# Row tiles in two banks for the transposes and the inverse width DFT of a spectral convolution block

## What is computed

```
def _L0_conv_ref(x, w1_real, w1_imag, w2_real, w2_imag):
    xf = jnp.fft.rfft2(x, norm='forward')
    top = jnp.einsum('bixy,ioxy->boxy', xf[:, :, :hm0, :hm1], w1)
    bot = jnp.einsum('bixy,ioxy->boxy', xf[:, :, -hm0:, :hm1], w2)
    out_fft = out_fft.at[:, :, :hm0, :hm1].set(top)
    out_fft = out_fft.at[:, :, -hm0:, :hm1].set(bot)
    return jnp.fft.irfft2(out_fft, s=(h, w), norm='forward')
...
x = x + _L0_conv_ref(_ln_c(x), ...)
t = _to_tokens(x)
t = t + _L0_ffn_ref(_ln_t(t), ...)
x = _from_tokens(t, x)
x = x + _L1_conv_ref(_ln_c(x), ...)
t = _to_tokens(x)
t = t + _L1_ffn_ref(_ln_t(t), ...)
x = _from_tokens(t, x)
```

## Time and profile before

| | |
|---|---|
| median of 3 runs | 623.37 us (618.92 to 623.65) |
| the profiled execution | 616.65 us |
| its span, first to last instruction | 614.8 us |
| TensorE matmuls busy | 572.2 us, 93% of the span |
| TensorE weight loads busy | 532.8 us, 87% |
| VectorE busy | 340.9 us, 55% |
| ScalarE busy | 315.9 us, 51% |
| GpSimd busy | 63.8 us, 10% |
| mean granted TensorE clock | 0.967 of full speed |

### The profile page before, as it was taken

The page is one execution under the profiler, slowest core; times in us unless marked ns, Lnnn a source line. Parts: engine busy times, 40 slices in busy tenths (PEclk is TensorE's granted clock), DMA queues, the critical chain, the costliest instruction groups (busy, mean ns, idle before and its releaser), DMA issues.

```text
span 614.8 us, 25791 instructions
## 1 busy us (share of the span) xinstructions
PE 572.2 (93%) x10936; PEld 532.8 (87%) x10936; DVE 340.9 (55%) x825; ACT 315.9 (51%) x791; POOL 63.8 (10%) x62
## 2 busy tenths in 40 slices
PE   8979799999997999997999999999999999966897
PEld 7979799999996987896999999989999999956773
DVE  3647666656469725564544444434544445498326
ACT  4766556642287302344555555576665555668400
POOL 4000000020021000000000003520000044710000
PEclk9989999999998979998999999999999999997779
DMA  9830782150000000000000004430000344300007
GB/s 353 328 136 2 276 298 117 37 238 1 2 1 1 2 20 1 0 1 1 4 0 0 3 3 109 109 40 4 0 0 3 58 81 75 64 0 1 2 3 273
DMA packets 48155, 40.74 MB, mean 66 GB/s; under 512 B 42553, under 2 KB 42809, under 8 KB 46876
## 3 DMA queue, kind: packets, MB, share of 16 engines
q1 hardware_dynamic: 46606, 37.27, 18.7%
q0 software_dynamic: 1344, 2.17, 1.7%
q10 hardware_dynamic: 144, 0.39, 0.2%
HBM read 27.49 MB, written 4.19 MB: 52 GB/s over the span
## 4 chain that ended last, share of the span: by engine, by line
PE 74%; DVE 11%; ACT 6%; POOL 2%; DMA 2%; issue 2%; SPq 2%; ACTq 0%; DVEq 0%
PE PS L732 32%; PE PS L443 6%; PE PS L696 5%; PE PS L518 5%; PE PS L464 3%; PE PS L646 3%; PE PS L725 2%; PE PS L593 2%; PE PS L542 2%; PE PS L502 2%; DVE sums L1042 2%; PE PS L549 2%; PE PS L563 2%; DVE RCD L1054 2%; SPq L329 2%
## 5 line engine op out<-in xcount | busy, mean ns | idle before, releaser
L732 PE MATMUL PS<-RE,conv_sb 128*64 128x64 f32 x6048 | 228.9, 227 | 2.0 <-DVE RE L1154 1.5
L732 PEld LDWEIGHTS PS<-RE,conv_sb 128*64 128x64 f32 x6048 | 211.2, 137 | 11.1 <-DVE RE L1154 3.7
L1154 DVE SCALAR_TENSOR_TENSOR RE<-PS,RE 128x64 f32<-128x64 f32 x504 | 113.2, 225 | 122.0 <-PE PS L732 111.3
L725 PE MATMUL PS<-ones_bf,biasT 128*64 128x64 bf16 x1008 | 100.4, 192 | 0.0
L865 ACT ACTIVATE RE<-RCD 128x128 f32 (+1 forms) x126 | 38.9, 310 | 53.7 <-DVE RE L1154 53.6
L725 PEld LDWEIGHTS PS<-ones_bf,biasT 128*64 128x64 bf16 x1008 | 59.9, 112 | 0.8
L464 PE MATMUL PS<-warm 128*128 128x128 bf16 x540 | 42.5, 250 | 8.6 <-ACT RCD L840 4.5
L464 PEld LDWEIGHTS PS<-warm 128*128 128x128 bf16 x540 | 39.3, 114 | 9.9 <-ACT RCD L840 4.7
L318 POOL DMA_DIRECT2D RE<-RCD x32 | 18.6, 588 | 200.7 <-ACT RCD L868 200.7
L929 DVE TENSOR_REDUCE sums<-RE 128x32 f32<-128x1024 f32 x16 | 19.4, 1218 | 33.3 <-ACT RE L772 33.3
L868 ACT COPY RB<-RE 128x128 f32 (+1 forms) x126 | 35.6, 283 | 1.5 <-DVE RE L1154 1.5
(11 more groups left out here) (125 smaller groups left out, 816.3 us busy)
## 6 DMA issues: line engine op xcount, KB each, us to landing
RE<-wspec SPq DMA_DIRECT2D x8, 2048.0 KB, 8.8
RA<-x_in SPq DMA_DIRECT2D x8, 512.0 KB, 7.6
RCD<-x_in SPq DMA_DIRECT2D x1, 4096.0 KB, 13.6
out<-RA SPq DMA_DIRECT2D x8, 512.0 KB, 2.7
RCD<-RB SPq DMA_DIRECT2D x48, 64.0 KB, 2.1
RCD<-RB SPq DMA_DIRECT2D x26, 32.0 KB, 1.9
conv_sb<-conv_w SPq DMA_DIRECT2D x1, 768.0 KB, 19.9
RE<-RCD SPq DMA_DIRECT2D x8, 96.0 KB, 4.1
```

The lines of the kernel that those rows point to most:

```text
L725: pe.matmul(conv_bank(u, h)[MO * o:MO * (o + 1)], biasT[:, s, MO * o:MO * (o + 1)], ones_bf[:, :], start=True, stop=False)
L732: m = pe.matmul(conv_bank(u, h)[MO * o:MO * (o + 1)], conv_sb[:, s, d, MO * o:MO * (o + 1)], prev, start=False, stop=(d == 2))
L1154: dve.scalar_tensor_tensor(out=state[:, state_slot(s, u), k, 1:1 + HO], in0=conv_bank(u, h), scalar=0.0, in1=rowb[:, u, k], op0=ALU.max, o ...
```

## The change

Where a block of 128x128 was transposed, or multiplied with `inv_w`, in one call, `row_tiles` now makes two: partitions 0 to 63 of the block and of the matrix, then 64 to 127. Each loads 64 rows by 128 columns and streams 64 columns of the matrix's own diagonal block; the first writes 64 columns in one bank, the second 64 in the next bank. So eight blocks still fill two banks, in another order, and the readers' access patterns follow it. This holds for the product transposes, `turn` (V and the image) and `dft_w_back`; `dft_h` stays as it was. Apart from that, VectorE's drain of the height DFT (`if2_pairs`) walks k innermost, so that it writes 8 neighbours at a time and reads PSUM 128 elements apart.

```
--- before.py
+++ after.py
@@ -215,18 +215,20 @@
 
         def t2_pairs(c):
             pairs = []
-            for bh in range(BH):
-                o = RB[:, :].rearrange("p (t k b o) -> p t b k o", t=BH, k=KY, b=BL)[:, bh, :, KYC * c:KYC * c + KYC]
-                i = turn_slot(c)[:, BANK * bh:BANK * (bh + 1)].rearrange("p (b y o) -> p b y o", b=BL, y=KYC)
+            for a in range(2):
+                y0 = KYC * c + 2 * a
+                o = RB[:, :].rearrange("p (t k b o) -> p t b k o", t=BH, k=KY, b=BL)[:, :, :, y0:y0 + 2]
+                i = turn_slot(c)[:, BANK * a:BANK * (a + 1)].rearrange("p (t b y o) -> p t b y o", t=BH, b=BL, y=2)
                 pairs.append((o, i))
             return pairs
 
         def if2_pairs(g):
-            o = RD.rearrange("p (t h r k) -> p t k r h", t=BH, h=H, r=2)[:, g % 2, 8 * (g // 2):8 * (g // 2) + 8]
-            return [(o, dft_slot(g).rearrange("p (k r h) -> p k r h", k=8, r=2))]
+            o = RD.rearrange("p (t h r k) -> p t r h k", t=BH, h=H, r=2)[:, g % 2, :, :, 8 * (g // 2):8 * (g // 2) + 8]
+            return [(o, dft_slot(g).rearrange("p (k r h) -> p r h k", k=8, r=2))]
 
         def t3_pairs(g):
-            return [(RB[:, 1024 * g:1024 * g + 1024], turn_slot(g))]
+            return [(RB[:, 1024 * g:1024 * g + 1024].rearrange("p (n a c) -> p n a c", n=8, a=2),
+                     turn_slot(g).rearrange("p (a n c) -> p n a c", a=2, n=8))]
 
         def xw_pairs(g, i):
             i = i.rearrange("p (b o i v) -> p i b o v", b=BL, o=4, i=Q)
@@ -417,6 +419,17 @@
 
         @block.tensor
         def _(pe):
+            def row_tiles(region, n, lhs, rhs):
+
+                for a in range(2):
+                    own = slice(MO * a, MO * (a + 1))
+                    out = region[:, BANK * a + MO * n:BANK * a + MO * (n + 1)]
+                    if rhs is None:
+                        m = pe.transpose(out, lhs[own], ident[own, own])
+                    else:
+                        m = pe.matmul(out, lhs[own], rhs[own, own], start=True, stop=True)
+                return m
+
             def group(j, ins, rhs):
 
                 for n, lhs in enumerate(ins):
@@ -539,14 +552,14 @@
                     if c >= 2:
                         pe.wait_ge(read, c - 1)
                     for x in range(X8):
-                        m = pe.transpose(blk(banks(4 * (c % 2) + 2 * w, 2), x), Z[:, c, x, w], ident)
+                        m = row_tiles(banks(4 * (c % 2) + 2 * w, 2), x, Z[:, c, x, w], None)
                     m.then_inc(full, 1)
 
             pe.wait_ge(s_tmp, NCH - 1)
 
             def turn(g, ins):
                 for n, lhs in enumerate(ins):
-                    m = pe.transpose(blk(turn_slot(g), n), lhs, ident)
+                    m = row_tiles(turn_slot(g), n, lhs, None)
                 m.then_inc(s_tf, 1)
 
             def turn_spectrum(c):
@@ -590,7 +603,7 @@
                 else:
                     pe.wait_ge(s_res, g - 1)
                 for n in range(8):
-                    m = pe.matmul(blk(dft_slot(g), n), blk(RB, 8 * g + n), inv_w, start=True, stop=True)
+                    m = row_tiles(dft_slot(g), n, blk(RB, 8 * g + n), inv_w)
                 m.then_inc(s_if1, 1)
 
             turn_image(0)
@@ -1015,8 +1028,8 @@
             for c in range(NCH):
                 dve.wait_ge(s_t0, c + 1)
                 dve.wait_ge(s_tmp, c + 1)
-                by_re = banks(4 * (c % 2), 2).rearrange("p (x a r n) -> p x a r n", x=X8, a=2, r=2)
-                by_im = imtmp[:, c % 2, :].rearrange("p (x a r n) -> p x a r n", x=X8, a=2, r=2)
+                by_re = banks(4 * (c % 2), 2).rearrange("p (a x r n) -> p x a r n", x=X8, a=2, r=2)
+                by_im = imtmp[:, c % 2, :].rearrange("p (a x r n) -> p x a r n", x=X8, a=2, r=2)
                 dve.tensor_tensor(V[:, c, :, :, 0, :], by_re[:, :, :, 0, :], by_im[:, :, :, 1, :], ALU.subtract)
                 dve.tensor_tensor(V[:, c, :, :, 1, :], by_re[:, :, :, 1, :], by_im[:, :, :, 0, :],
                                   ALU.add).then_inc(s_comb, 1)
@@ -1029,8 +1042,9 @@
             dve.wait_ge(s_xr, 16)
             for g in range(8):
                 dve.wait_ge(s_if1, g + 1)
-                x1 = RC[:, 1024 * g:1024 * g + 1024]
-                dve.tensor_tensor(x1, dft_slot(g), x1, ALU.add).then_inc(s_res, 1)
+                x1 = RC[:, 1024 * g:1024 * g + 1024].rearrange("p (n a w) -> p n a w", n=8, a=2)
+                image = dft_slot(g).rearrange("p (a n w) -> p n a w", a=2, n=8)
+                dve.tensor_tensor(x1, image, x1, ALU.add).then_inc(s_res, 1)
 
             def experts(l):
 
```

## The result

| | median, us | runs | profiled execution, us | its span, us |
|---|---|---|---|---|
| before | 621.99 (616.18 to 623.65) | 13 | 616.65 | 614.8 |
| changed | 614.76 (609.63 to 618.18) | 13 | 615.30 | 613.5 |

The ratio is 0.9894, 95% interval 0.9859 to 0.9928: 1.1% faster, 6.6 us. Forecast were 5.5 us and a time of 617.9 us, with a range of 611 to 627; the median is 614.76. The 3.1 us between them are in part the start of the sum: three runs gave 623.37 us for the kernel before, thirteen give 621.99. Ratios and intervals here leave out executions more than 1.5% above the quickest of their kernel; medians are of all.

The account below looks back on a forecast made before the run. TensorE was taken to bound the 59 us of touched stretches. Gains of 3.0, 0.3, 2.8 and 0.95 us less losses of 1.0 and 0.5 gave -5.5 us, from the 623.37 us median to 617.9, range 611 to 627.

Parts of the forecast that it names:

- Products: Product transposes as row tiles: VectorE's combining operations become late next at 1.31 us a chunk; gain 3.0 us.
- V transposes: 64 transposes of V as row tiles: strided load of 0.108 us sets the pace; gain 0, at most 3.3 us.
- Inverse width DFT: 64 blocks as row tiles: two loads of 0.108 us in turn, 0.216 against 0.223 a block; gain about 0.3 us.
- Image transposes: 64 contiguous transposes around the width DFT: a group of eight falls from 0.88 to 0.47 us; gain 2.8 us.
- Height drain: VectorE's drain of the height DFT falls from 1.95 to 1.25 us, removing TensorE waits; gain 0.95 us.
- Changes of form: TensorE alternating between row tiles and full array around the height DFT: three round trips of 0.34 us; loss 1.0 us.
- Instructions: 256 more transposes and 128 more matmul records may leave TensorE idle; loss 0.5 us, bounds 0 and 3.5.
- Rival A: Loads of the two row groups go one after the other on TensorE: 20.7 us slower, 644 us; chance 0.18.
- Rival B: TensorE loads cheaper than durations suggest, V and width DFT gain, no idle gap: gain 9.0 us, 614 us; chance 0.26.
- rival C: Gain eaten: height drain stays at 1.95 us and two 1.7 us gaps appear; gain 1.6, 622 us; chance 0.18.

Follow-up runs that it names:

- the contiguous variant: Changed kernel with V's transposes reading contiguous blocks instead of columns 8 elements apart; first V transpose to first image transpose took 20.8 us instead of 23.1.
- the variant without them: Changed kernel with V's transposes as whole blocks again; first V transpose to first image transpose 22.3 us, whole kernel 607.36 us, ratio 0.976 to the kernel before.
- the four-tile kernel: Changed kernel with whole V transposes and the inverse width DFT as four 64 x 64 tiles a block; 604.21 us, ratio 0.982 to the kernel before.

## Why the prediction was right

**Products.** Forecast 3.0 us, measured 3.4. The step held: VectorE is late next and sets the pace. The term was small because a chunk takes 1.24 us, not the 1.31 that I made of 1.29 and an allowance: with no wait between chunks, the next first operation too starts 0.60 to 0.70 after its predecessor. VectorE's first operation came 1.87 us after the first transpose instead of 2.25, 0.38 sooner, where 0.4 was forecast.

**V transposes.** Forecast 0, measured 0: 0.055 us a record, 0.110 a block before and after. The bound named, a load of 128 columns read with a stride, was shown by the contiguous variant.

**Inverse width DFT.** Forecast 0.3, measured 0. The bound was right (the variants with fewer columns loaded and streamed show it), but the load occupies 0.109 to 0.110 us rather than 0.108. I also hadn't counted the seams: some 0.05 us from each group to the transposes, and 0.1 from the last group into keep_warm.

**Image transposes.** Forecast 2.8, measured 2.6 with the width DFT in it: six groups 0.38 sooner each (0.41 forecast), the start 0.38. A group takes 0.50 us where 0.47 was forecast.

**Height drain.** Duration forecast 1.25, measured 1.22; worth 0.95 forecast, 0.84 measured.

**Changes of form.** Forecast a loss of 1.0 us in V and height. Measured 0.20 in and 0.14 out, the very prices of the mix, and 0.8 us in the variant without them. That this loss and the drain's gain cancel is why the middle stretch stands still at 23.1.

**Instructions.** Forecast a loss of 0.5 us; no such idle time of the matmul queue shows in these stretches, so 0 in this profile. It came in the four-tile kernel, at 0.017 us a record; that the rate is what brings it is not shown.

Sum of the stretches: 3.4 + 0.0 + 2.6 + 0.1 (between keep_warm and the first projection) = 6.05, against 5.5. That they lie so close is in part luck: the products gave 0.4 us more than forecast and the instructions cost 0.5 less, while image and width together gave 0.5 less, and those errors cancel. The whole kernels show a gain but not its size (ratios of 0.989 and 0.995 in two comparisons), so it is the stretches that bear the mechanism out. Rival A was refuted in its own terms: its prices appeared when both tiles shared rows, and nowhere else. Rival B's cheaper loads didn't appear; only its missing idle gap did. Of rival C neither half happened in the changed kernel.

What I had weak was the footing: I took one profiled execution and three runs, and didn't see that the profiled one was an execution with a high clock in its last stage. The forecast was made as a difference and so survived; a comparison of the two spans, 1.3 us apart, would have denied the gain.

## What to carry to other kernels

Before cutting a matmul into row tiles, find which of its two halves sets the pace: tiles side by side halve the stream but not the load of 128 columns, so contiguous transposes gained nearly half, while strided ones and fp32 matmuls gained nothing. Count the changes between tiled and whole instructions (0.34 us a round trip here), and keep neighbours in the same form even where the form itself brings nothing. Where the clock varies between executions, compare the touched stretches, or runs at equal clock, not two spans.

## What the runs showed of the hardware

- Loads in different row groups run side by side, and in the same row group they don't: an fp32 block of two row tiles cost 0.22 us in the first case, 0.46 at clock 1.00 and 0.85 at 0.50 in the second.
- Four tiles of 64 x 64 go side by side as well, 0.017 us a record, but with four gaps without a releaser, 3.0 us of idle in 18.7. Their cause is open.
- TensorE can be busy all of a stretch by its records and yet be granted half the clock: with the row tiles of the width DFT all on rows 0 to 63 the clock went from 1.00 to 0.50 at about 158.6 us and stayed there until 220, and when row tiles streamed 32 columns instead of 64 it was 0.50 from 143.7 to 170.8 us. The same tiles on both row groups with 64 columns kept 1.00 in all five profiles that have them. Each of the two is one execution, and the clock also fell for 3 us in a variant whose code there was the changed kernel's, so it is not shown that the thinner stream or the shared rows brought it down.
- VectorE's copy from PSUM to SBUF in runs of 8 elements took 1.22 us for 1024 elements, against 1.95 for single elements 256 bytes apart; it read PSUM 128 elements apart and was still no longer than the residual add of 1024 elements, 1.23.
